# Deltas of x over all 512 tokens on TensorE's row tiles, in a mixture-of-LoRA kernel on one Trainium2 core

## The reference

```python
# layer 0: one adapter per batch
Bx  = einsum('bni,bri->bnr', x, B0[adapter_ids])
x   = x + einsum('bnr,bor->bno', Bx, A0[adapter_ids])
# layer 1: a dense matrix and top-2 gated experts
base   = einsum('btd,od->bto', x, W)
logits = einsum('btd,ed->bte', x, Wr) + 5.0 * one_hot(language_ids)
gates  = scatter(softmax(top_k(logits, 2)))
h      = einsum('btd,erd->bter', x, A)
x      = x + base + 2.0 * einsum('bter,bte,eor->bto', h, gates, B)
```

## Time and profile before

| what | value |
|---|---|
| median of 3 runs | 1550.69 us (1549.33 to 1550.87) |
| the profiled execution's own time | 1550.23 us |
| its span in the trace | 1548.4 us |
| PE busy | 99% of the span, 7430 matmuls |
| DVE, ACT, POOL busy | 79%, 46%, 5% |
| granted TensorE clock, mean | 0.998 |

### The profile page before, as it was taken

How to read it: one execution, slowest core, us unless ns; L and a number is a source line. 1 busy time by engine, 2 the same in 40 slices (tenths; PEclk the granted TensorE clock), 3 DMA queues, 4 the chain that set the end, 5 groups by cost and what they waited for, 6 DMA issues and landing times.

```text
span 1548.4 us, 20276 instructions
## 1 busy us (share of the span) xinstructions
PE 1537.9 (99%) x7430; PEld 1294.5 (84%) x7430; DVE 1228.3 (79%) x1694; ACT 714.1 (46%) x911; POOL 77.2 (5%) x118
## 2 busy tenths in 40 slices
PE   9999999999999999999999999999999999999999
PEld 9778888888888888888888888888888888888887
DVE  6998879976788768887698776997769976787665
ACT  6532223554445444454445454454444554445443
POOL 2333231000000000000000000000000000000000
PEclk9999999999999999999999999999999999999999
DMA  9899997877767767687666876668767776666564
GB/s 262 225 282 289 297 253 248 219 224 200 237 224 223 213 207 230 199 246 214 208 218 201 250 210 218 217 205 233 204 215 237 214 212 197 215 220 216 203 218 163
DMA packets 303110, 347.04 MB, mean 224 GB/s; under 512 B 204891, under 2 KB 236683, under 8 KB 302347
## 3 DMA queue, kind: packets, MB, share of 16 engines
q1 hardware_dynamic: 270978, 307.46, 66.7%
q0 software_dynamic: 9136, 30.94, 5.9%
q10 hardware_dynamic: 22896, 7.35, 2.2%
HBM read 278.52 MB, written 66.72 MB: 223 GB/s over the span
## 4 chain that ended last, share of the span: by engine, by line
PE 94%; DVE 3%; ACT 0%; issue 0%; ACTq 0%; DMA 0%; SPq 0%; POOL 0%; DVEq 0%; POOLq 0%
PE pb L804 28%; PE pb L806 28%; PE pb L805 28%; PE pb L378 5%; PE pb L380 2%; PE pb L533 2%; DVE raw L684 1%; DVE xl L558 1%; PE pb L319 1%; DVE pool_a L540 1%; ACTq L292 0%; DMA a0g<-a0p 0%; DVE wl L800 0%; PE pb L1060 0%; PE pb L417 0%
## 5 line engine op out<-in xcount | busy, mean ns | idle before, releaser
L796 ACT CAST wh<-raw 128x1024 fp32r<-128x1024 f32 (+1 forms) x453 | 475.1, 1049 | 701.9 <-PE pb L806 637.8
L800 DVE TENSOR_TENSOR wl<-raw,wh 128x1024 fp32r<-128x1024 f32 (+1 forms) x453 | 551.8, 1218 | 253.6 <-ACT wh L796 252.5
L804 PE MATMUL pb<-wh,sh 128*128 128x512 f32 x1568 | 617.8, 394 | 0.0
L806 PE MATMUL pb<-wh,sl 128*128 128x512 f32 x1568 | 611.9, 390 | 0.0
L805 PE MATMUL pb<-wl,sh 128*128 128x512 f32 x1568 | 610.4, 389 | 0.0
L806 PEld LDWEIGHTS pb<-wh,sl 128*128 128x128 f32 x1568 | 294.2, 188 | 64.1
L805 PEld LDWEIGHTS pb<-wl,sh 128*128 128x128 f32 x1568 | 294.9, 188 | 55.7
L804 PEld LDWEIGHTS pb<-wh,sh 128*128 128x128 f32 x1568 | 294.4, 188 | 54.5
L378 PE MATMUL pb<-awb,xah 128*128 128x304 f32 x512 | 136.9, 336 | 0.2 <-DVE aux L395 0.2
L380 PE MATMUL pb<-awb,xal 128*128 128x152 f32 x512 | 119.2, 233 | 0.0
L804 PE MATMUL pb<-wh,xh 128*128 128x512 f32 x256 | 101.3, 396 | 0.8 <-DVE xl L558 0.8
(11 more groups left out here) (154 smaller groups left out, 1251.8 us busy)
## 6 DMA issues: line engine op xcount, KB each, us to landing
raw<-t_scr SPq DMA_DIRECT2D x392, 512.0 KB, 3.8
xst<-in_x_dram SPq DMA_DIRECT2D x368, 64.0 KB, 3.6
out_dram<-ost SPq DMA_DIRECT2D x66, 256.0 KB, 3.3
raw<-in_L_cond_W_dram SPq DMA_DIRECT2D x124, 128.0 KB, 5.6
raw<-bt_scr SPq DMA_DIRECT2D x28, 512.0 KB, 3.5
out_dram<-u SPq DMA_DIRECT2D x56, 256.0 KB, 2.9
t_scr<-raw POOLq DMA_DIRECT2D x32, 256.0 KB, 4.8
t_scr<-tst POOLq DMA_DIRECT2D x16, 512.0 KB, 7.0
```

Source lines behind the costliest of these rows:

```text
L796: e.copy(pair_split(wh, g), pair_source(g)).then_inc(c_wh, 1)
L800: e.tensor_tensor(out=pair_split(wl, g), in0=pair_source(g), in1=pair_split(wh, g).bitcast(f32), op=ALU.subtract).then_inc(c_wl, 1)
L804: e.matmul(o, h, wh[:, g % RING, k, :], start=start, stop=False)
L806: return e.matmul(o, l, wh[:, g % RING, k, :], start=False, stop=stop)
```

## The change

For batches 2 to 7 a pair of feature tiles (16 deltas a batch become 8 pairs) is done by two matmuls of 64 rows and 512 columns: the first with rows 0 to 63 of `a0g` and `bxt`, the second with rows 64 to 127, each into a bank of its own. For this, rows 64 to 111 of `bxt` repeat Bx (in all batches), and rows 64 to 111 of `a0g` repeat A0's rows by three more DMAs (batches 2 to 7). Pairs stand in slots 44, 47, 48, 50, 52, 54, 56, 58, the two adapts of a pair in its slot and the one after.

```diff
+        def st_columns(at):
+            return st48[:, :, :].rearrange("p t (g c) -> p t g c", g=2)[:, :, :, at:at + R]
+
+        def bx_twice():
+            return aux[:, :, NAUX:AW].unsqueeze(2).to_broadcast([P, TT, 2, R])
+
         def bx_hi(e, n):
             e.wait_ge(c_gd, GD * n + 2)
-            e.copy(st48[:, :, 0:R].bitcast(f32r), aux[:, :, NAUX:AW]).then_inc(c_ga, 1)
-            e.copy(st48[:, :, 2 * R:3 * R].bitcast(f32r), aux[:, :, NAUX:AW]).then_inc(c_ga, 1)
+            for at in (0, 2 * R):
+                e.copy(st_columns(at).bitcast(f32r), bx_twice()).then_inc(c_ga, 1)
 
         def bx_lo(e, n):
             e.wait_ge(c_ga, GA * n + 4)
-            e.tensor_tensor(out=st48[:, :, R:2 * R], in0=aux[:, :, NAUX:AW], in1=st48[:, :, 0:R], op=ALU.subtract)\
-             .then_inc(c_gd, 1)
+            e.tensor_tensor(out=st_columns(R), in0=bx_twice(), in1=st_columns(0), op=ALU.subtract).then_inc(c_gd, 1)
...
+        def wide_bank(p):
+            return (6, 4)[p % 2]
+
+        def delta_wide(e, n, p):
+            a, kp = divmod(p, KP)
+            if p == 0:
+                e.wait_ge(c_ga, GA * n + 5)
+                e.wait_ge(c_x1, 16 * n)
+            elif p == 1:
+                e.wait_ge(c_gd, GD * n + 5)
+            else:
+                e.wait_ge(c_x1, 16 * n + 2 * p - 2)
+            for k in range(2):
+                at = (a * HK + 2 * kp + k) * P
+                rows = slice(64 * k, 64 * k + 64)
+                e.matmul(pb[:, wide_bank(p) + k, :], a0g[rows, at:at + P], bxt[rows, :],
+                         start=True, stop=True).then_inc(c_dl, 1)
+
+        def adapt_wide(e, n, p, half):
+            a, kp = divmod(p, KP)
+            e.wait_ge(c_dl, 16 * n + 2 * p + 2)
+            quads = quarter(n, a + 2 * half)[:, 2 * kp:2 * kp + 2, :]
+            e.tensor_tensor(out=quads, in0=quads,
+                            in1=pb[:, wide_bank(p):wide_bank(p) + 2, half * HT:(half + 1) * HT], op=ALU.add)\
+             .then_inc(c_x1, 1)
...
-            else:
+            elif b == 1:
                 e.wait_ge(c_x1, 16 * b + 4 * SUM_QUARTER[product] + kp + 1)
+            else:
+                e.wait_ge(c_x1, 16 * b + (2 * kp + 1 if product == 0 else 16))
...
+        WIDE_AT = (44, 47, 48, 50, 52, 54, 56, 58)
...
+            if n >= 2:
+                for row, part in G_ROWS:
+                    e.dma_start(a0g[64 + row:64 + row + R, 0:D].bitcast(f32), a_scr[part, n * R:(n + 1) * R, 0:D])\
+                     .then_inc(d_ag, 16)
...
-                        if i >= 44:
-                            delta(e, n, i - 44)
+                        if i in WIDE_AT:
+                            delta_wide(e, n, WIDE_AT.index(i))
...
-                        if i >= 44:
-                            adapt(e, n, i - 44)
+                        for p, half in ADAPT_AT.get(i, ()):
+                            adapt_wide(e, n, p, half)
```

More of the change, by code:

```diff
@@ L429, in aux_adapted @@
             e.wait_ge(c_ga, GA * n + 5)
-            e.wait_ge(d_ag, 48 * n + 48)
+            e.wait_ge(d_ag, 48 + 48 * n + 48 * max(n - 1, 0))
             if n == 0:
@@ L595, in sum_hi @@
                 e.wait_ge(c_add, 8 * (b - 1) + SUM_READY[product] + kp // 2 + 1)
+            elif b == 1:
+                e.wait_ge(c_x1, 16 * b + 4 * SUM_QUARTER[product] + kp + 1)
             else:
-                e.wait_ge(c_x1, 16 * b + 4 * SUM_QUARTER[product] + kp + 1)
+                e.wait_ge(c_x1, 16 * b + (2 * kp + 1 if product == 0 else 16))
             if b == 1 and product == 0:
@@ L997, in adapted_moe_lora_kernel @@
                 SPLIT_AT[at] = (product + 1, kp)
+        WIDE_AT = (44, 47, 48, 50, 52, 54, 56, 58)
+        ADAPT_AT = {}
+        for p, at in enumerate(WIDE_AT):
+            for half in range(2):
+                ADAPT_AT.setdefault(at + half, []).append((p, half))
         DELTAS0 = {0: (4, 5), 1: (6, 7), 2: (8, 9), 3: (10, 11), 4: (12, 13), 5: (14, 15)}
```

## The result

The changed kernel takes 1558.11 us (median of 6 runs, 1555.01 to 1562.3), the kernel before 1550.20 us (6 runs, 1549.24 to 1550.87): 1.005 of its time, 95% interval 1.0039 to 1.006. In a second group of runs it was 1556.31 us (8 runs) beside 1550.89: 1.0038, interval 1.0021 to 1.0056. Forecast were 1560.7 us, and slower with a chance of 0.66. One execution of all groups (the kernel before, beside two_pairs_moved and full_pairs_again) ran at a granted clock of 0.752, took 1890.38 us and is left out of the ratios.

The account below looks back on a forecast made before the run. PE bounds the kernel, busy 99% of the span. Pairs +11.5 us (0.72 each for two deltas' 0.48, 48 times), slot 49's wait -1.6, Bx twice +0.6: +10.5 on 1550.2, 1560.7 us; range 1542 to 1567.

Parts of the forecast that it names:

- The direction and the mechanism: Slower, chance 0.66: at each change of rows around a pair, the weight load waits until the matmul before is nearly done.
- part of a drain: Rival for the pairs: one change of rows free, or the bare loads hidden; 1551.1 us, chance 0.10.
- no drain: Rival: 64-row loads made under the matmul before, halves at work together; 1537.2 to 1542.5 us, chance 0.20.
- the second load: In each pair, the second weight load and matmul come 0.11 us behind the first if the halves overlap.
- The bare load: At each change of rows, a weight load not hidden under a matmul costs PE 0.10 us.
- The wait in slot 49: A delta's weight load there waited for an adapt in batches 2 to 7; the change removes it, -1.6 us.
- Bx twice: Writing Bx's second copy, casts in slot 41 and `bx_lo`: +0.4 us in seven batches, +0.2 in batch 0.
- The DMAs: 18 more DMAs for A0's rows, issued in slot 25: hidden, nothing on PE; 7.8 us without that cover.
- The rival of the halves in turn: Drain, and a pair's two matmuls one after the other: pair 0.84 us, +16.3, 1566.5 us, chance 0.14.

Follow-up runs that it names:

- two_pairs_moved: Changed kernel with its eight pairs a batch two behind one another, in slots 47, 50, 54 and 57: 1545.72 us beside 1550.75, ratio 0.9963.
- full_pairs_again: full_pairs run once more, unedited: 1548.49 us beside 1550.75, ratio 0.998.
- full_pairs: Changed kernel with its slots, banks and 512-column matmuls, but each on all 128 rows, Bx and A0's rows not held twice: 1547.70 us, ratio 0.9975.
- dmas_alone: Kernel before plus only the 18 more DMAs and the wait for them, rows 64 to 127 of `bxt` zero: 1550.33 us, ratio 0.9992.
- bx_twice_alone: Kernel before plus only the changed kernel's `bx_hi` and `bx_lo`, rows 64 to 127 of `a0g` zero: 1550.34 us, ratio 0.9999.
- four_banks_alone: Kernel before with the deltas of batches 2 to 7 over four banks from the fifth on: 1549.34 us beside 1550.89, ratio 0.9982.
- halves_in_turn: Changed kernel with both matmuls of a pair on rows 0 to 63, A0's rows not held twice: 1568.05 us beside 1550.50, ratio 1.0108.

## Why the prediction was right, point by point

**The direction and the mechanism held.** The two changes of rows at the kernel's start told what 64 rows do. The load 0.07 before the end of the matmul ahead gave 0.32 us, and 0.32 was measured, in every pair behind a full matmul. full_pairs shows that the rows cause it, with dmas_alone and bx_twice_alone for what else it takes away. The drain is there in both directions; "part of a drain" and "no drain" have fallen.

**The step that was mis-sized is the second load.** It was put 0.11 us behind the first, by two loads of full weights; a pair came to 0.72. In the changed kernel the two loads go to different halves and are made at once (0.19 for both), the second matmul starts 3 to 4 ns behind the first, and a pair takes 0.63, a little over what the sum gives without that term, 0.61. Forecast were +0.24 a pair and +11.5 us for 48, measured are 0.63 - 0.48 = +0.15, +7.2 us. The Trainium skill, page "TensorE: Matmul & The Clock Gate", Part 3, has a load overlapping with matmuls under way only where the row groups differ, and the tiles' matmuls starting about 4 ns apart. The 4 ns agree with the trace, and I had set them beside the no-drain rival only, not in the sum. The "only" does not fit here: loads on all 128 rows start with the 128-row matmul before them (412.60). Without the term of the second load the sum would have been 48 x (0.19 + 0.42 - 0.48) = +6.2 for the pairs, and 1555.4.

**The bare load** was forecast at 0.10 and is 0.11 behind the pair (0.34 - 0.23).

**The wait in slot 49** went and did not come back: -1.6 us forecast, and four_banks_alone, which takes away nothing else, has 185.87 - 185.60 = 0.27 a batch, -1.6.

**Bx twice** was forecast at +0.6, of which 0.4 were for seven batches and 0.2 for batch 0. bx_twice_alone's marks give +0.6 for six batches alone, 0.10 each for 0.06 forecast; the part of batch 0 was not measured. `bx_lo` takes 285 ns for 0.284 forecast, and PE's waits for it went from 2.3 us to 2.8:

```profile
L411 DVE TENSOR_TENSOR st<-aux,st x8: 284/285/293, 43.3 to 1331.3; 128x128 f32<-128x128 f32 x8
...
  PEld pb L422: 2.8, 7
```

**The DMAs** are hidden, as forecast.

Together: +7.2 - 1.6 + 0.6 = +6.2; the marks give +6.1, the profiled execution +5.9 (1556.09 for 1550.23). The median of the first group lies 2 us higher. The two traces have 186.88 and 186.87 a batch, so nothing in the traced executions puts that part into the batches. What differs between traced executions lies in the first batch, for other kernels too: dmas_alone's profiled execution (1557.5 us) has its first mark at 278.43, 7.1 us later than before, and its batches as usual. Its trace shows why (the chain, PE's timeline, and a stretch with the granted clock, the third number from the end):

```profile
237.47 13.29 DMA raw<-in_L_cond_W_dram
...
250.94 0.39 PE L806 MATMUL pb<-wh,xl 128*128 128x512 f32 x1
255.49 0.79 PE L533 MATMUL pb<-bxt,a0g 128*128 128x256 f32 x2 [4.16 <-DVE pool_a L540]
...
253.50:260.20 6.70, 4.71 (x13) 3.84 (x14) 6.55 (x21) 1.61 (x4) 1.97 (x3) 0.50 0.76 232
```

A piece of W landed 13.29 us after its issue, where the median of these DMAs is 5.3 there; DVE came late with the work behind it, PE started no matmul between 250.94 and 255.49, and the granted clock then was 0.50 (1.2 GHz) up to 260.2, full matmuls 0.43 apart instead of 0.23. bx_twice_alone's profiled execution (1556.39 us) shows the same in another place: 13.59 us for a piece, no matmul started between 119.05 and 123.03, and from 121.5 to 128.2 a granted clock of 0.50 with full matmuls 0.43 apart. The 18 added DMAs aren't the cause: the first of them is issued at 355.9. Why a piece lands late in some executions stays open, and the slow executions of the changed kernel (up to 1562.3 us) have no trace; the second group's +5.4 fits that the delay falls on kernels by chance.

**What was luck.** The six batches cost +6.1 us for the +10.5 forecast. The first group's median is at +7.9, nearer to the forecast, by time that the traces don't show in the batches. And the stated range, 1542 to 1567 us, took in both signs: that the time fell into it says little; what bears the forecast out is the 0.32 and the 0.11 in the trace.

**The rival of the halves in turn** has fallen by its own experiment, and its price was right: +16.3 forecast for the kernel, +17.0 by halves_in_turn's marks.

## What to carry to other kernels

Row tiling pays by the visit, not by the matmul. Here a change of rows costs about 0.2 us each way, drain and bare load, against 0.24 us of work saved by a pair's overlap; one pair between full-array matmuls loses 0.15 us, two pairs in one visit win 0.11. So put tiled matmuls together (two pairs, on four PSUM banks, were tried here, more were not), and look in the trace of the kernel as it is for any matmul with another number of rows: the start of the weight load behind it, measured from the start of the matmul before, shows the drain before anything is built.

Where a visit stands can turn it from a gain to a loss: two visits moved by one slot gave 0.42 us a batch here. In a kernel with repeated batches the distance between like instructions tells 0.02 us where medians of a dozen runs tell 1 to 2.

## What of the hardware was not expected

- Two weight loads of 64 rows in different halves took 0.19 us together, as one; in the same half 0.29, one behind the other.
- The drain stands at 0.32 us behind a 512-column matmul and at the same 0.07 before the modelled end for 128 rows to 24, 24 to 128, 128 to 64 and 64 to 128.
- In two traces PE started no matmul for 4.6 and 4.0 us behind a piece of W that landed after more than 13 us; the granted clock was 0.50 after that, and full matmuls stood 0.43 us apart.
- Two 512-column matmuls on all 128 rows behind one another took 0.47 us in full_pairs, not 0.454, 0.235 for each where those of the main loop take 0.227. Why was not tried.
